# The second operand of a residual: a bias added by GpSimd's arithmetic, or by DMAs that GpSimd issues

## The reference

```
cond(x):   out[b] = W[condition[b]]^T @ x[b]         # a 64x64 matrix picked for each b
layer 0:   x = x + cond0(x) @ ternary(w0) + b0       # w0 is 1024x1024; ternary: sign where |w| >= 0.05, times a column scale
layer 1:   x = x + cond1(x) @ (nf4(q) * scale)^T + bias1 + 4 * (cond1(x) @ A^T) @ B^T
```

## Time and profile before

| what | us |
|---|---|
| median of 3 executions | 372.79 |
| lowest and highest of them | 370.15, 373.74 |
| the profiled execution, its own time | 371.03 |
| its span, first to last instruction | 369.2 |
| PE busy | 354.6 |
| DVE, ACT, POOL busy | 243.3, 169.6, 228.3 |

### The profile page before, as it was taken

One profiled execution on the slowest core, in us unless ns is written; L12 is line 12 of the kernel. 1 busy time (PEld: TensorE's weight loads), 2 busy tenths in 40 slices (PEclk: granted clock), 3 DMA queues, 4 the chain that ended last, 5 costly groups with the idle time before them and its releaser, 6 DMA issues.

```text
span 369.2 us, 5527 instructions
## 1 busy us (share of the span) xinstructions
PE 354.6 (96%) x1832; PEld 299.9 (81%) x1832; DVE 243.3 (66%) x361; ACT 169.6 (46%) x302; POOL 228.3 (62%) x147
## 2 busy tenths in 40 slices
PE   7999987999999999998989999999999999999996
PEld 6788875878888888887868888888888888888885
DVE  4996457587997887974699999846155362544522
ACT  4775647678888778882021323504013040231300
POOL 0769999956886878667443302386468464685642
PEclk9999999899999999999999999999999999999999
DMA  7994400554246146333331133021405014150202
GB/s 212 309 306 142 148 22 29 193 211 146 96 167 199 45 156 216 117 114 114 127 119 57 61 120 114 18 101 62 174 36 180 22 70 166 57 175 4 114 30 85
DMA packets 27838, 44.63 MB, mean 121 GB/s; under 512 B 8834, under 2 KB 17026, under 8 KB 27810
## 3 DMA queue, kind: packets, MB, share of 16 engines
q1 hardware_dynamic: 26466, 43.95, 34.9%
q10 hardware_dynamic: 1344, 0.33, 0.4%
HBM read 27.49 MB, written 16.78 MB: 120 GB/s over the span
## 4 chain that ended last, share of the span: by engine, by line
PE 73%; DVE 10%; ACT 6%; issue 4%; POOL 4%; DMA 1%; SPq 1%; DVEq 0%; POOLq 0%; ACTq 0%
PE acc L1177 31%; PE acc L1139 20%; PE xT L1103 9%; PE acc L1119 7%; PE spare L1103 3%; DVE plain_sums L927 3%; ACT spare L721 2%; POOL x_first L557 2%; DVE side_p L908 2%; DVE hl L865 2%; ACT hh L673 1%; PE acc L1204 1%; DMA mix<-in_L_cond_weights 1%; PE acc L1103 1%; POOL side_p L584 1%
## 5 line engine op out<-in xcount | busy, mean ns | idle before, releaser
L551 POOL TENSOR_TENSOR X<-X,bias 128x1024 f32<-128x1024 f32 x28 | 69.1, 2468 | 34.1 <-PE xT L1103 26.6
L1139 PE MATMUL acc<-T,hh 128*128 128x512 f32 x192 | 75.9, 396 | 0.0
L1139 PE MATMUL acc<-T,hl 128*128 128x512 f32 x192 | 75.0, 391 | 0.0
L721 ACT ACTIVATE spare<-q_mid 128x512 f32<-128x512 int8 x96 | 55.5, 596 | 13.6 <-DVE side_p L908 6.6
L1177 PE MATMUL acc<-W,hh 128*128 128x512 f32 x192 | 61.1, 389 | 0.0
L1103 PEld LDWEIGHTS xT<-mix,X 128*128 128x128 f32 x352 | 43.7, 197 | 7.4 <-issue 6.4
L1103 PE MATMUL xT<-mix,X 128*128 128x128 f32 x352 | 44.6, 282 | 4.2 <-DVE hl L865 4.1
L1010 DVE TENSOR_TENSOR X<-X,acc 128x512 f32<-128x512 f32 x36 | 24.7, 687 | 32.9 <-PE acc L1177 18.6
L1177 PEld LDWEIGHTS acc<-W,hh 128*128 128x128 f32 x192 | 36.0, 188 | 7.5
L1139 PEld LDWEIGHTS acc<-T,hl 128*128 128x128 f32 x192 | 36.1, 188 | 7.4
L1139 PEld LDWEIGHTS acc<-T,hh 128*128 128x128 f32 x192 | 36.1, 188 | 7.0
(11 more groups left out here) (97 smaller groups left out, 662.5 us busy)
## 6 DMA issues: line engine op xcount, KB each, us to landing
out<-X SPq DMA_DIRECT2D x26, 512.0 KB, 3.1
X<-out SPq DMA_DIRECT2D x16, 512.0 KB, 3.4
X<-in_x SPq DMA_DIRECT2D x12, 512.0 KB, 3.4
q_raw<-in_L_ffn_q_weight SPq DMA_DIRECT2D x16, 256.0 KB, 2.9
w_in<-in_L_ffn_w SPq DMA_DIRECT2D x15, 256.0 KB, 5.2
x_first<-in_x SPq DMA_DIRECT2D x4, 512.0 KB, 5.2
out<-x_first SPq DMA_DIRECT2D x4, 512.0 KB, 5.8
out<-X SPq DMA_DIRECT2D x4, 256.0 KB, 2.0
```

What stands on the lines that cost most here:

```text
L551: pool.tensor_tensor(x_of(g), x_of(g), bias[:, :], ALU.add).then_inc(s_xb, 1)
L721: act.activation(dst, q_mid[:, parity, :], ACT.Copy, scale=slope, bias=offset).then_inc(s_line, 1)
L1139: mm = pe.matmul(acc[:, bank_of(q), :], a[:, k, :], b, start=(k == 0 and j == 0), stop=(k == KB - 1 and j == len(terms) - 1))
```

## The change

All additions of a bias are DMAs from the bias to x, with an addition at the destination. GpSimd issues each where its arithmetic instruction stood, with the same waits ahead of it; what follows on GpSimd may then start at once unless it waits for the DMA. Each slot of X has its own semaphore now, and who waited for s_xb waits in `biased` for that of the slot. The second bias has a tensor of its own, and SyncE loads it in the round of tile 4, behind the spills of tiles 0 to 3 and with no wait of its own. The last piece of weights is turned after q = 30 and no longer after q = 29. The banks of q = 32 to 39 move by one: q = 32 has bank 0 and no longer bank 3, and q = 39 bank 3 and no longer bank 2.

```diff
     def turned_in(d):
-        return max(NH * F, ready_in(d) + 1)
+        return max(NH * F, ready_in(d) + (2 if d == ND - 1 else 1))
     def bank_of(q):
         if q >= NH * NT:
-            return (q + 3) % F
+            return q % F
...
+        bias1 = sb("bias1", [P, T], F32)
...
-        s_xb = sem("s_xb")
+        s_xb = [sem(f"s_xb{k}") for k in range(XS)]
...
+        def biased(eng, g):
+            eng.wait_ge(s_xb[g % XS], 16 * (g // XS + 1))
...
                     for t in range(F):
                         spill(t)
+                    sp.dma_start(bias1[:, :], b1.rearrange("(a f) -> a f", a=1).to_broadcast([P, T])
+                                 ).then_inc(s_b1, 16)
...
-            sp.wait_ge(s_xb, NT)
-            sp.dma_start(bias[:, :], b1.rearrange("(a f) -> a f", a=1).to_broadcast([P, T])
-                         ).then_inc(s_b1, 16)
...
             def add_bias(g):
                 arrived(pool, g)
                 pool.wait_ge(s_b1 if g >= NT else s_b0, 16)
                 pool.wait_ge(s_xT, NH * (g + 1))
-                pool.tensor_tensor(x_of(g), x_of(g), bias[:, :], ALU.add).then_inc(s_xb, 1)
+                pool.dma_start(x_of(g), (bias1 if g >= NT else bias)[:, :], accum_op=ALU.add
+                               ).then_inc(s_xb[g % XS], 16)
             def result_half(q):
                 t, n = q % F, q // F
-                pool.wait_ge(s_xb, t + 1)
+                biased(pool, t)
                 pool.wait_ge(s_ys, q + 1)
                 pool.tensor_tensor(half(t, n), half(t, n), ys[:, t, :], ALU.add).then_inc(s_res0, 1)
             def result(g):
-                pool.wait_ge(s_xb, g + 1)
+                biased(pool, g)
...
# and in the same way biased(...) for s_xb in add_sum (POOL), leave_y and take (DVE)
```

More of the change, by code:

```diff
@@ L605, in add_sum @@
                 which, tile, n = SUMS[i]
-                pool.wait_ge(s_xb, SB + 2 * p + tile + 1)
+                biased(pool, SB + 2 * p + tile)
                 pool.wait_ge(s_take, taken(p, 2 + which))
@@ L887, in leave_y @@
                     g = q // NH
-                    dve.wait_ge(s_xb, g + 1)
+                    biased(dve, g)
                     dve.tensor_tensor(half(g, n), half(g, n), acc[:, bank_of(q), :], ALU.add
@@ L1001, in take @@
                     return
-                dve.wait_ge(s_xb, SB + 2 * p + tile + 1)
+                biased(dve, SB + 2 * p + tile)
                 earlier = [b for b in range(a) if TAKES[b][1:] == (tile, n)]
```

## The result

The changed kernel takes 385.12 us (median of four runs, 381.62 to 389.04), the kernel before 372.26 (370.15 to 373.74, the same three runs and one more). The ratio is 1.032, with a 95% interval of 1.027 to 1.038: slower, by 12.9 us where 9.3 were forecast (the forecast time, 382.1, started from a median of 372.79 and is 3.0 us short). The profiled execution took 389.04 us with a span of 387.2; it is the longest of the four and counts as a slow run, which the ratio leaves out, so I take places and durations from it, and what a term is worth from medians of other runs as well. What its stands and shifts add up to is its own span, +18.0 us, and not the 12.9 of the medians.

What follows compares the result with a forecast made beforehand. TensorE, busy 354.6 of 369.2 us, was taken as the bound. Terms 11.4 - 0.7 - 2.2 - 0.6 + 1.4 = +9.3 us on the profiled 371.03, with the median 1.8 higher, gave 382.1 us; range 375.5 to 395.

Steps and rivals of the forecast that it cites:

- The start: GpSimd's row before weight(1) ends: four DMA round trips waited for at once, 5.8 us each, replace 2.47 us instructions; +11.4 us.
- S: Shift of the end of weight(1) on GpSimd from four waited round trips and a fifth bias's issue; +11.4 us.
- The last piece: TensorE's stand at 168.87: mixed(16) now comes first, held only by low_x(15, 1); -0.7 us.
- Arithmetic off GpSimd: Layer 1: VectorE's sums no longer collide with GpSimd's additions; -2.2 us at mixed(18) and -0.6 us for later small stands.
- the rival of the lock: Issuing DMAs shuts VectorE out as GpSimd's arithmetic does; 388.7 us, chance 0.08.
- The banks: First product now waits for leave_y(39) on VectorE, a new TensorE stand; +1.4 us, at least 1.0, at most 5.2.
- Costed at nothing: Later tiles and pairs: bias waits hidden; delayed loads of x issued over 15 us before their mixed; no cost.

Runs made afterwards that it cites:

- e2: Changed kernel, but GpSimd issues the four bias DMAs of tiles 0 to 3 in a row, ahead of the first result_half; 376.15 us, no ratio given.
- e5: Changed kernel, but plain 512 KB SBUF-to-SBUF moves replace the adding DMAs of tiles 0 to 3 (b0 left out there); 376.63 us, single execution.
- e8: As e7, but biases of tiles 2 and 3 are DMAs issued ahead of tile 0's arithmetic, tile 4's a DMA in place; 364.65 us, ratio 0.982.
- e9: Changed kernel, but in each round of layer 0 SyncE issues the spill and load of x ahead of the q_raw loads; 384.15 us, ratio 1.032.
- e1: Changed kernel, but biases of tiles 0 to 3 are added by GpSimd's arithmetic again, all others by DMA; 372.47 us, ratio 1.001.
- e3: Kernel before, arithmetic biases kept, with only the banks of q = 32 to 39 moved and the last piece turned later; 374.2 us, ratio 1.007.
- e12: As e8, but the biases of tiles 16 to 31 (layer 1) are added by GpSimd's arithmetic again; 364.65 us, ratio 0.981.
- e7: As e6, but the seven products take banks 0, 1, 2, 3, 0, 1, 2; 368.25 us, ratio 0.991.
- e6: Changed kernel, but all 16 biases of layer 0 are added by arithmetic, those of layer 1 by DMA; 369.98 us, ratio 0.995.
- e10: Changed kernel, but SyncE issues the spill and load of x ahead of q_raw only in rounds from tile 5 on; 380.8 us, ratio 1.022.

## Why the prediction was right, and where it was not

The direction, the place and the main mechanism held: four round trips in a row, each waited for at once. The time (385.1 against 382.1) lies in the range. One step failed, the delay of x that was costed at nothing, and two terms came out right in size with something wrong inside. Term by term, in the profiles:

**The start.** S was forecast as +11.4. The row after is 40.9 - 29.6 = 11.3 us longer, from the four waits (22.5 where I had 4 x 5.8 = 23.2), the issue (0.6 where I had 0.5) and half a microsecond of smaller gaps and longer instructions; the other 1.3 us by 76.56 are there before the first bias, which starts at 35.59 in this run and at 34.5 to 34.8 in e2, e5, e8 and e9. The agreement is luck in part, for it hides two errors. The quiet trip is 4.5 us, not 5.8: I priced the second stream at 2.2 us, and e5 against it says 1.55. And the trips are not alike: the first took 8.5 us beside the loads of x, an end that I had left to the range. I had also expected the stand at `turn_w(1)` to grow; it shrank to 2.58, and the wait stood ahead of `mixed(5)` instead, but GpSimd's `weight(1)` still came last, so the sum was the same. e1 shows that this term is the loss, and e2 and e8 that it is the wait and not the DMA: with all four issued in a row `weight(1)` ends 12.1 us earlier than in the changed kernel, and with two issued ahead and two biases by arithmetic 16.7 us earlier.

**The last piece.** Forecast -0.7, with `mixed(16)` held by `low_x(15, 1)`. `mixed(16)` goes from +19.0 to +17.9, and `mixed(17)`, behind the piece, is at 196.91 for 178.45, +18.5: -0.5. In e3, which has the same edit in the kernel before, it is -0.6. Right.

**Arithmetic off GpSimd.** Forecast -2.8 in two parts. Between `mixed(17)` and `mixed(20)` (234.95 for 219.01, +15.9) the changed kernel wins 2.5, so the size is right, but the reason that I gave is not the whole of it. GpSimd's arithmetic does collide with VectorE's sums, and an issue doesn't, which also ends the rival of the lock:

```profile
212.40 0.88 POOL L557 DMA_DIRECT2D X<-bias  x1 [11.00 <-PE xT L1110]
...
212.14 0.68 DVE L934 TENSOR_TENSOR plain_sums<-W 128x512 f32<-128x512 f32 x1
212.86 0.69 DVE L934 TENSOR_TENSOR plain_sums<-plain_sums,W 128x512 f32<-128x512 f32 x1
```

But e12 keeps the arithmetic and collisions and loses nothing. In the kernel before three of GpSimd's additions ran in a row against VectorE, because the first had waited 7.31 us for the second bias, and held three sums for 8.3 us; in e12, where the second bias is there early, the first is done by 172.6, two are left, and the three sums take 5.2. So the bias tensor of its own was enough to take the stand at 193 away. No run changes that tensor alone, and e12 has other edits ahead of this place; it is the nearest there is. I had named both edits in the step and priced only the one.

**The banks.** Forecast +1.4, with 1.0 and 5.2 as bounds; measured 2.05 in the changed kernel and 1.7 as the gain of taking it away (e7 against e6). The term was 0.3 to 0.6 us too small. I had put 7.3 us from the end of `leave_y(38)` to the end of `leave_y(39)` (227.7 to 235.0); in the profile after it is 7.7, from 242.97 + 0.68 to 250.71 + 0.68 = 251.39, where the first product starts at 251.44.

**Costed at nothing, and wrong.** "The loads of x that they could delay are issued more than 15 us before their `mixed`" was the step that failed. I hadn't looked it up. In the kernel before the load of x for tile 10 is issued at 102.70, since SyncE stood until 99.00 with a q_raw ahead of the spill, and `mixed(10)` starts at 106.64: 3.9 us, of which this load takes 3.3. Here are the rows of that kernel that I should have read:

```profile
91.79 7.16 SPq L444 DMA_DIRECT2D q_raw<-in_L_ffn_q_weight  x2
99.00 0.51 SPq L449 DMA_DIRECT2D out<-X  x1
102.70 0.34 SPq L434 DMA_DIRECT2D X<-in_x  x1
```

The load of tile 10 goes into the slot that the spill of tile 6 empties, and is issued when that spill has landed. So in the kernel before there were 3.9 - 3.3 = 0.6 us of slack. In the changed kernel the load is issued at 116.97, lands 6.1 us later, and `mixed(10)` starts at 123.10. In the traces that keep SyncE's order the DMA view of the two transfers, issue to landing, gives (us):

| run | biases of tiles 5 to 15 | spill | load | both, less 7.0 | stand ahead of `mixed(10)` |
|---|---|---|---|---|---|
| before, e6, e8 | arithmetic | 3.7 | 3.3 | 0 | none |
| e1 | DMAs | 4.8 | 4.0 | 1.8 | 1.28 |
| e5 | DMAs | 5.2 | 4.7 | 2.9 | 2.45 |
| changed kernel | DMAs | 5.3 | 6.1 | 4.4 | 3.84 |
| e2 | DMAs | 5.6 | 5.9 | 4.5 | 4.00 |

The stand is what the two transfers take longer, less the 0.6 us of slack, to within 0.2 us in each of them: 4.4 - 0.6 = 3.8 in the changed kernel. The additions share the 16 DMA engines with these transfers (23.6% of the span beside 33.1%), and of these seven traces only the ones that have them in these rounds have the longer transfers. The stand and the slow clock behind it are 6.4 us of the profiled run (+12.6 to +19.0) and some 4 us of the medians (e10), about what the forecast fell short by (3.0). Without them e10 is 9.3 us slower than the kernel before, and 9.3 was the sum that I had made. That the two agree to the tenth is luck: e10's interval reaches from 5.9 to 10.4 us, its own profile is 11.5 us longer than the one before, and the errors above offset each other.

What stays open: why the same 28 DMAs stretch these two transfers by 1.8 us in e1 and by 4.4 in the changed kernel. q_raw, the spills and the additions meet in another order there, and I made no run that moves one of them alone. How much of a median the slow clock makes, apart from the stands that precede it, is open too.

## What to carry to other kernels

A DMA in place of an engine's instruction exchanges occupancy for latency: the engine is free sooner, and the result is there later. It pays where the engine has other work between the issue and the first use, and loses where the next instruction in the list is the one that waits; so look at what stands right behind it, in program order, before counting freed busy time. Here 32 exchanges cost 3%, and three of them, two issued 10 us ahead of need, gave 1% (e8 against e7, which adds all biases of layer 0 by arithmetic).

When a change adds transfers, look for the tightest load that is there already and measure its slack from its issue to its use, not from its place in the code: a queue that waits for something else on the way decides when it goes out.

## What the runs showed of the hardware that I had not expected

A DMA that adds 512 KB from SBUF to SBUF takes 4.5 us from GpSimd's issue to the waiting instruction when it is alone, a plain one 2.95. Its issue holds GpSimd for 0.88 us by the profile, the plain one's for 0.58, and the next instruction starts 0.6 us after the first begins (70.71, 71.32). The Trainium skill, "DMA: Bandwidth & Descriptors" (Anatomy of one DMA), gives 2.0 us plus bytes over 436 GB/s for one issued by GpSimd, 3.2 us for 512 KB; the plain 2.95 is near it. For two streams that gives 4.4, by my estimate, and 4.5 were measured. I had put 1 us on top of it for the first byte and come to 5.4; the page lists that latency, but doesn't add it to its 2.0 us, and the trip shows no room for it.

Of four such DMAs issued in a row, three took 2.8 us together and the fourth began 3.9 us later (e2). A limit on what GpSimd can have outstanding would look like this; no run here varies it, so the cause is not shown.

In the 4 us or so that follow a stand, TensorE's granted clock was 0.50 behind the stands of 11.2 and 3.8 us, and 0.59 behind the 2.58 us at 76.56, where the 16 loads of `mixed(6)` took 3.32 us; in the kernel before it was 0.57 behind the 3.04 us at 63.94. Behind stands of 2.18 (193.27, before) and 1.1 us (187.23, after) it was 1.00. The length of the stand alone doesn't tell: behind 2.31 us in e3 (192.78) it was 0.72 and behind 2.45 us in e5 (113.35) 1.00.
